# Copying the split Q and K parts and the shift rows straight between SBUF tiles, from two queues, in a two-layer block on one core

## The chip, the cores and the metric

The kernel runs on one core of one Trainium2 chip. The metric is the device time of one execution in microseconds (us); lower is better. Engines are called by the profile's names: PE (TensorE), DVE (VectorE), ACT (ScalarE), POOL (GpSimd), SP (SyncE). SPq and POOLq are the instruction queues from which SP and POOL issue DMAs.

## The reference, cut to what matters

Batch B = 2, sequence S = 512, width D = 128, 16 heads of width 8. Two attentions follow each other for each batch element; both need scores in a precision near float32.

```python
x = x + ffn0(cond_scale(cond, x))                    # quantised feed-forward, inner 512
# first attention: causal, one more key and value made from cond ("image")
q, k, v = split(x @ c_attn_w + c_attn_b)
scores = q k^T / sqrt(8); softmax over 512 keys and the image key
a1 = (softmax @ v) @ c_proj_w + c_proj_b
# second attention: not causal, over a1, then its own projection
q, k, v = split(a1 @ in_proj_w.T + in_proj_b)
a2 = mha(q, k, v) @ out_proj_w.T + out_proj_b
x3 = layernorm(a1 + a2)
out = x + layernorm(x3 + moe(x3))                    # 8 experts, width 256, top 1
```

## The kernel before, in words

The kernel is written by engine: each engine's block walks over one list of steps, ORDER, and executes its share of each step `(name, a, i)`. ORDER is made by `program_order()` from a table of begin, middle and end times written out by hand; within an engine the instructions run in that order. `a` counts the attentions ("instances"): 0 and 1 are the first attention of the two batch elements, 2 and 3 the second; `b = a % 2`. Engines synchronise by semaphores. Line numbers are those of the profile.

**Split into three parts.** Q and K are computed in float32 as 128 rows (8 dims x 16 heads) by 512 positions. Since PE's fast matmul takes bf16, each is split into three bf16 parts: the high part is a cast on ACT (L730 for Q, L736 for K), the middle and low parts are the casts of the rest on DVE (L936 to L938, L942 to L944). They lie in `Qp` and `Kp`, 128 rows by 3 parts by 512.

**Stacks.** A score matmul contracts over 72 rows: three parts of Q times three parts of K times 8 dims. `Qs` holds each part of Q three times in a row (rows 24n to 24n+23 for part n), `Ks` holds the three parts of K in sequence, three times. Each row is one (part pair, dim) and goes over 16 heads by 512 positions. So heads, which are rows in `Qp`, must become columns in `Qs`. Before, that is done by way of DRAM, all of it from SP in the step "v": L514 and L516 write `Qp` and `Kp` (384 KB each) to DRAM tensors; then, for each half of the heads, three DMAs of L526 bring 24 rows each of `Qs`, and three of L533 24 rows each of `Ks` (192 KB each, contiguous runs of 8 KB). That makes 12 DMAs of 192 KB for an instance, 2.36 MB.

**Who waits.** The step "scores" (L1209 on PE) computes 64 score blocks for an instance. Block 0 waits for the first half of the stacks, block 32 for the second half. For each block DVE takes a row maximum (L959). In instance 0 the order runs blocks 0, 1 and 2 and then block 32 as the fourth.

**Shift rows.** From the maxima of 8 heads DVE makes the negated maximum in two bf16 parts, PE transposes it (L1224), ACT copies it to `nmT` (16 rows by 512, L739). SP sends it to DRAM (L538), waits until it is there, and brings it into rows 72 and 73 of `Qs` (L540). Attention of those 8 heads ("attend", L1235) waits for that.

**Rows 72 to 76 at the start.** 14 small DMAs from SBUF to SBUF (L504 to L509, 1 KB runs, one to three destination rows each, 320 KB in all, issued from 22.35 to 33.25 us) fill the constant rows of the stacks in the step "prepare".

Of the kernel before, what the change touches and what calls it, by code (L numbers as in the profile page):

```python
# [17 lines left out]
P = 128  # L18
# [20 lines left out]
INST = 4  # L39
# [187 lines left out]
def two_layers(nc, A, out):  # L227
# [17 lines left out]
    with ctx:  # L245
# [6 lines left out]
        def sem(name):  # L252
            return ctx.enter_context(nc.semaphore(name))


        parts_dram = [[nc.dram_tensor(f"parts_{n}{a}", (PARTS, P, S), bf16, kind="Internal").ap()
                       for n in "qk"] for a in range(INST)]
        shift_dram = [nc.dram_tensor(f"shift_{a}", (2, HEADS, S), bf16, kind="Internal").ap()
                      for a in range(INST)]


        ident = sb("ident", [P, P])
        identb = sb("identb", [P, P], bf16)
        causal_q = sb("causal_q", [P, P], bf16)
# [170 lines left out]
        y_ready = sem("y_ready")  # L435
        r2_ready = sem("r2_ready")
        qhi_ready, khi_ready = sem("qhi_ready"), sem("khi_ready")
        qp_ready, kp_ready = sem("qp_ready"), sem("kp_ready")
        parts_q = [sem(f"parts_q{a}") for a in range(INST)]
        parts_k = [sem(f"parts_k{a}") for a in range(INST)]  # L440
        stacked = [[sem(f"stacked{a}_{n}") for n in range(2)] for a in range(INST)]
        mparts_ready, bias_ready = sem("mparts_ready"), sem("bias_ready")
        half_done = sem("half_done")
        fixed_rows = sem("fixed_rows")
# [1 line left out]
        nm_ready = sem("nm_ready")  # L446
        simg_ready, pimg_ready, zimg_ready = sem("simg_ready"), sem("pimg_ready"), sem("zimg_ready")
        turned_ready, residual_ready = sem("turned_ready"), sem("residual_ready")
        shift_out = [sem(f"shift_out{a}") for a in range(INST)]
        shifted = [[sem(f"shifted{a}_{g}") for g in range(2)] for a in range(INST)]  # L450
        ve_ready, rstd_ready, gained = sem("ve_ready"), sem("rstd_ready"), sem("gained")
        x3_ready = sem("x3_ready")
        dl_ready, ex_ready = sem("dl_ready"), sem("ex_ready")
        comb_ready = sem("comb_ready")
        out_ready, stored = sem("out_ready"), sem("stored")

        block = ctx.enter_context(nc.Block())

# [2 lines left out]
        def _(sp):  # L461
            for step, a, i in ORDER:
# [47 lines left out]
                                     orow[:, :].unsqueeze(1).to_broadcast([PARTS, HEADS, S])).then_inc(fixed_rows, 16)  # L510
                if step == "v":

                    sp.wait_ge(qp_ready, a + 1)
                    sp.dma_start(parts_dram[a][0].rearrange("n p s -> p n s"), Qp[:, :, :]).then_inc(parts_q[a], 16)  # L514
                    sp.wait_ge(kp_ready, a + 1)
                    sp.dma_start(parts_dram[a][1].rearrange("n p s -> p n s"), Kp[:, :, :]).then_inc(parts_k[a], 16)  # L516


                    row, count = HEADS * S, HEADS // 2 * S
                    for half in range(2):  # L520
                        heads = slice(half * HEADS // 2, (half + 1) * HEADS // 2)
                        sp.wait_ge(parts_q[a], 16)
                        for n in range(PARTS):
                            r = n * PARTS * HD
                            src = parts_dram[a][0][n]
                            sp.dma_start(Qs[r:r + PARTS * HD, b, heads, :].rearrange("p h s -> p (h s)"),  # L526
                                         bass.AP(tensor=src.tensor, offset=src.offset + half * count,
                                                 ap=[[0, PARTS], [row, HD], [1, count]])).then_inc(stacked[a][half], 16)
                        sp.wait_ge(parts_k[a], 16)
                        src = parts_dram[a][1]  # L530
                        for n in range(PARTS):
                            r = n * PARTS * HD
                            sp.dma_start(Ks[r:r + PARTS * HD, b, heads, :].rearrange("p h s -> p (h s)"),  # L533
                                         bass.AP(tensor=src.tensor, offset=src.offset + half * count,
                                                 ap=[[row, PARTS * HD], [1, count]])).then_inc(stacked[a][half], 16)
                if step == "max_rows":
                    sp.wait_ge(free["misc"], filled("misc", "max_rows", a, i))
                    sp.dma_start(shift_dram[a][i], nmT[:, b, i, :]).then_inc(shift_out[a], 16)  # L538
                    sp.wait_ge(shift_out[a], 16 * (i + 1))
                    sp.dma_start(Qs[SHIFT:SHIFT + 2, b, i * HALF:(i + 1) * HALF, :].rearrange("p h s -> p (h s)"),  # L540
                                 shift_dram[a][i].rearrange("(n h) s -> n (h s)", h=HALF)).then_inc(shifted[a][i], 16)
                if step == "load_experts":

                    sp.wait_ge(full["t1"], filled("t1", "weights", 2, UNITS - 1))
# [10 lines left out]
        def _(pool):  # L555
# [9 lines left out]
            for step, a, i in ORDER:  # L565
# [44 lines left out]
                if step == "turn_weights":  # L610

                    pool.wait_ge(r1_ready, 1)
                    pool.wait_ge(in_mask, 16)
                    then_wait(pool.tensor_scalar(mparts[:, 0, :], mrow[:, :], 1.0, None, ALU.mult))
                    then_wait(pool.tensor_tensor(mres[:, :], mrow[:, :], mparts[:, 0, :], ALU.subtract))
                    then_wait(pool.tensor_scalar(mparts[:, 1, :], mres[:, :], 1.0, None, ALU.mult))
                    pool.tensor_tensor(mparts[:, 2, :], mres[:, :], mparts[:, 1, :], ALU.subtract)\
                        .then_inc(mparts_ready, 1)
                    pool.wait_ge(in_att, 16 * 17)
                    pool.tensor_tensor(brow[:, 2, :], brow[:, 2, :], brow[:, 3, :], ALU.add)\  # L620
                        .then_inc(bias_ready, 1)
                if step == "max_rows" and a < 2:

                    pool.wait_ge(pimg_ready, NTH[step, a, i])
                    pool.wait_ge(perm_ready, 1)
                    pool.wait_ge(free["s0"], filled("s0", "image_v"))
                    heads, shape = slice(i * HALF, (i + 1) * HALF), [P, NT, HALF, HD + 1]
                    pool.tensor_tensor(Zimg[:, b, :, heads, :], Vimg[:, b, heads, :].unsqueeze(1).to_broadcast(shape),
                                       Pimg[:, b, :, heads].unsqueeze(3).to_broadcast(shape),
                                       ALU.mult).then_inc(zimg_ready, 1)  # L630
# [13 lines left out]
        def _(act):  # L644
# [4 lines left out]
            for step, a, i in ORDER:  # L649
# [70 lines left out]
                if step == "q":  # L720
                    if a >= 1:

                        act.wait_ge(parts_q[a - 1], 16)
                        act.wait_ge(parts_k[a - 1], 16)
                    act.wait_ge(perm_ready, 1)
                    ps = take("misc", "q", a)
                    act.activation(Qf[:, b, :], ps[:, :], ACT.Identity, bias=cols5[:, 0:1] if a < 2 else bjoin[:, 0:1],
                                   scale=float(HD) ** -0.5).then_inc(free["misc"], 1)
                    act.wait_ge(free["misc"], filled("misc", "q", a))
                    act.activation(Qp[:, 0, :], Qf[:, b, :], ACT.Copy).then_inc(qhi_ready, 1)  # L730
# [49 lines left out]
        def _(dve):  # L780
# [39 lines left out]
            for step, a, i in ORDER:  # L820
# [112 lines left out]
                if step == "q":  # L933

                    dve.wait_ge(qhi_ready, a + 1)
                    then_wait(dve.tensor_tensor(qres[:, :], Qf[:, b, :], Qp[:, 0, :], ALU.subtract))  # L936
                    then_wait(dve.tensor_copy(Qp[:, 1, :], qres[:, :]))
                    dve.tensor_tensor(Qp[:, 2, :], qres[:, :], Qp[:, 1, :], ALU.subtract).then_inc(qp_ready, 1)  # L938
                if step == "k":

                    dve.wait_ge(khi_ready, a + 1)
                    then_wait(dve.tensor_tensor(kres[:, :], Kf[:, :], Kp[:, 0, :], ALU.subtract))  # L942
                    then_wait(dve.tensor_copy(Kp[:, 1, :], kres[:, :]))
                    dve.tensor_tensor(Kp[:, 2, :], kres[:, :], Kp[:, 1, :], ALU.subtract).then_inc(kp_ready, 1)  # L944
                if step == "v":
                    if a < 2:
                        dve.wait_ge(stack_init, 2)
# [126 lines left out]
        def _(pe):  # L1074
# [6 lines left out]
            for step, a, i in ORDER:  # L1081
# [114 lines left out]
                        mm = pe.matmul(ps[:, t * D:(t + 1) * D], x[:, b, t * P:(t + 1) * P], w, start=True, stop=True)  # L1196
                    mm.then_inc(full["misc"], 1)
                if step == "scores":
                    if i == HEADS * NT // 2:
                        pe.wait_ge(stacked[a][1], 16 * 2 * PARTS)  # L1200
                    if i == 0:
                        pe.wait_ge(stacked[a][0], 16 * 2 * PARTS)
                        if a < 2:
                            pe.wait_ge(fixed_rows, 16 * 2 * (PARTS + 3))
                    rows = MASK + PARTS if a < 2 else STACK
                    h, t = i // NT, i % NT
                    ps = put(SCORES[a, i], "scores", a, i)
# [153 lines left out]
```

## Time and profile before

| | |
|---|---|
| Time, median of 3 runs | 475.95 us (471.48 to 479.54) |
| Profiled execution, span from the first to the last instruction | 480.0 us |
| Busy in the span | PE 361.9, DVE 257.0, ACT 172.7, POOL 28.7 us |
| Share of the chain that ended last | PE 53%, DVE 15%, DMA 14% |
| Bytes moved by DMA | 18.59 MB |

No other time is given for the profiled execution; its span of 480.0 us lies 0.85% above the median of the runs. Busy time tells how long an engine executed, not what held it up; what held it up is in the waits and in the chain of work that ended last.

### The profile page before, as it was taken

What the parts mean: (1) busy time and instruction counts of PE and PEld (TensorE: products, weight loads), DVE (VectorE), ACT (ScalarE), POOL (GpSimd) and SP (SyncE); (2) the same over time, 40 slices, a digit from 0 to 9 for tenths busy, and PEclk for the clock granted to TensorE, in tenths of its full rate; (3) what the DMA queues carried; (4) which work ended last, traced back from release to release, by engine and by line L of the source; (5) the groups of instructions that cost most, each with busy time, mean ns of one, the idle gap of its engine ahead of it and who ended that gap; (6) DMA issues with size and microseconds to landing.
All of it is one profiled execution on the core that took longest, in us unless ns stands there. A gap on an engine that the chain in (4) does not pass through costs nothing.

```text
span 480.0 us, 5378 instructions
## 1 busy us (share of the span) xinstructions
PE 361.9 (75%) x2027; PEld 176.0 (37%) x2028; DVE 257.0 (54%) x630; ACT 172.7 (36%) x245; POOL 28.7 (6%) x52
## 2 busy tenths in 40 slices
PE   0358633698599987719978947999969999688992
PEld 0134221254345443304322312222433535465771
DVE  4672841699367552204598634567755223336644
ACT  2542320201234456604511751465625674112120
POOL 9600000000000000000000000000010000100000
PEclk9996575657579897955995885589988999869898
DMA  6210441061000000530000251000500000000000
GB/s 179 27 25 2 115 94 55 33 145 72 18 1 3 5 0 4 136 88 41 1 0 4 79 118 68 3 0 18 161 0 4 1 0 1 0 1 1 22 1 22
DMA packets 12092, 18.59 MB, mean 39 GB/s; under 512 B 1261, under 2 KB 10193, under 8 KB 10899
## 3 DMA queue, kind: packets, MB, share of 16 engines
q1 hardware_dynamic: 11778, 17.98, 13.9%
q0 software_dynamic: 288, 0.28, 0.6%
q8 instruction: 16, 0.26, 0.2%
q14 instruction: 10, 0.07, 0.1%
HBM read 14.13 MB, written 3.80 MB: 37 GB/s over the span
## 4 chain that ended last, share of the span: by engine, by line
PE 53%; DVE 15%; DMA 14%; issue 8%; ACT 5%; SPq 3%; POOL 0%; POOLq 0%; DVEq 0%; ACTq 0%
PE ps_pv L1253 11%; DMA Ks<-parts_k 11%; PE ps_t L1235 9%; PE ps_s L1209 9%; DVE mx L959 6%; PE ps_s L1322 4%; PE ps_misc L1330 4%; DMA shift<-nmT 2%; SPq L526 2%; PE ps_misc L1187 2%; PE ps_misc L1264 1%; PE ps_t L1238 1%; ACT probs L764 1%; PE ps_t L1209 1%; PE ps_s L1212 1%
## 5 line engine op out<-in xcount | busy, mean ns | idle before, releaser
L959 DVE TENSOR_REDUCE mx<-ps_s 128x1 f32<-128x512 f32 (+3 forms) x219 | 121.9, 585 | 96.7 <-PE ps_s L1209 59.1
L764 ACT ACTIVATE probs<-ps_t 128x1024 f32<-128x1024 f32 (+2 forms) x128 | 107.8, 864 | 115.0 <-PE ps_t L1238 62.8
L1209 PE MATMUL ps_s<-Ks,Qs 72*128 72x512 bf16 (+4 forms) x219 | 88.4, 428 | 50.2 <-DMA Ks<-parts_k 34.1
L1235 PE MATMUL ps_t<-Qs,Ks 74*128 74x512 bf16 (+4 forms) x256 | 81.5, 392 | 7.4 <-DMA Qs<-shift 5.2
L1209 PEld LDWEIGHTS ps_s<-Ks,Qs 72*128 72x128 bf16 (+1 forms) x219 | 23.6, 111 | 120.7 <-DVE mx L959 53.6
L1253 PE MATMUL ps_pv<-probs,Vs 128*32 128x512 f32 (+3 forms) x512 | 65.6, 589 | 1.4 <-ACT probs L764 1.4
L1235 PEld LDWEIGHTS ps_t<-Qs,Ks 77*128 77x128 bf16 (+1 forms) x256 | 27.0, 110 | 46.8 <-issue 24.0
L1330 PE MATMUL ps_misc<-Ks,shared 128*128 128x128 f32 x256 | 34.6, 292 | 6.2 <-DVE shared L810 2.8
L1330 PEld LDWEIGHTS ps_misc<-Ks,shared 128*128 128x128 f32 x256 | 33.1, 205 | 12.4 <-issue 10.9
L1060 DVE SCALAR_TENSOR_TENSOR shared<-ps_misc,comb,shared 128x128 f32<-128x128 f32 x64 | 18.0, 344 | 32.6 <-PE ps_misc L1330 32.6
L1322 PE MATMUL ps_s<-Qf,Ks 128*128 128x512 f32 x64 | 31.8, 621 | 0.0
L1238 PE MATMUL ps_t<-causal_k,identb 128*128 128x128 bf16 x128 | 28.0, 245 | 0.0
L1212 PE MATMUL ps_s<-causal_q,identb 128*128 128x128 bf16 x100 | 26.1, 265 | 0.0
L750 ACT ACTIVATE shared<-ps_s,cols 128x512 f32<-128x512 f32 x16 | 11.0, 687 | 39.7 <-PE ps_s L1322 39.7
L634 POOL TENSOR_TENSOR rstd<-ve,halves 128x4 f32<-128x4 f32 x4 | 4.2, 1040 | 286.6 <-DVE ve L804 286.6
L739 ACT ACTIVATE nmT<-ps_misc 16x512 bf16<-16x512 bf16 x8 | 4.7, 585 | 43.4 <-PE ps_misc L1224 43.4
L959 DVE TENSOR_REDUCE mx<-ps_t 128x1 f32<-128x512 f32 (+3 forms) x37 | 20.2, 585 | 0.0
L1253 PEld LDWEIGHTS ps_pv<-probs,Vs 128*32 128x32 f32 x512 | 11.1, 113 | 22.5 <-issue 20.4
L1051 DVE TENSOR_SCALAR shared<-ps_s,cols 128x512 f32<-128x512 f32 x16 | 11.9, 746 | 13.3 <-PE ps_s L1322 13.3
L1209 PE MATMUL ps_t<-Ks,Qs 77*128 77x512 bf16 (+4 forms) x37 | 16.1, 463 | 1.5 <-DVE mx L959 1.0
L1322 PEld LDWEIGHTS ps_s<-Qf,Ks 128*128 128x128 f32 x64 | 12.0, 206 | 9.7 <-issue 9.4
L1238 PEld LDWEIGHTS ps_t<-causal_k,identb 128*128 128x128 bf16 x128 | 14.3, 112 | 2.4 <-issue 1.8
(237 smaller groups left out, 348.8 us busy)
## 6 DMA issues: line engine op xcount, KB each, us to landing
Qs<-parts_q SPq DMA_DIRECT2D x24, 192.0 KB
Ks<-parts_k SPq DMA_DIRECT2D x24, 192.0 KB
parts_q<-Qp SPq DMA_DIRECT2D x4, 384.0 KB, 2.5
parts_k<-Kp SPq DMA_DIRECT2D x4, 384.0 KB, 2.6
Ks<-in_L_ffn_w SPq DMA_DIRECT2D x1, 1024.0 KB, 5.8
X<-in_x SPq DMA_DIRECT2D x2, 256.0 KB, 4.3
out_x<-shared SPq DMA_DIRECT2D x2, 256.0 KB, 2.3
shared<-in_L_ffn_w_gate SPq DMA_DIRECT2D x1, 256.0 KB, 4.8
```

The lines of the kernel that those rows point to most:

```text
L750: act.activation(hid[:, i % 2, 1, :], ps[:, :], ACT.Relu, bias=cols17[:, 2 * i + 1:2 * i + 2])\
L764: act.activation(probs[:, half % 2, j, 0:w], ps[:, 0:w], ACT.Exp).then_inc(free[f"t{i % 2}"], 1)
L959: dve.tensor_reduce(mx[:, b, t, h:h + 1], ps[:, 0:w], AX, ALU.max).then_inc(free[SCORES[a, i]], 1)
L1051: dve.tensor_scalar(hid[:, i % 2, 0, :], ps[:, :], cols17[:, 2 * i:2 * i + 1], 0.0, ALU.add, ALU.max).then_inc(free["s0"], 1)
L1060: last = dve.scalar_tensor_tensor(out=acc[:, a, t, :], in0=ps[:, t * D:(t + 1) * D], scalar=comb[:, a, t, i // 2, i % 2:i % 2 + 1], in1=ac ...
L1209: mm = pe.matmul(ps[:, 0:w], Qs[0:rows, b, h, t * P:(t + 1) * P], Ks[0:rows, b, h, 0:w], start=True, stop=(a >= 2))
L1212: mm = pe.matmul(ps[:, w - P:w], identb[:, :], causal_q[:, :], start=False, stop=True)
L1235: mm = pe.matmul(ps[:, col:col + w], Ks[0:rows, b, h, kb * P:(kb + 1) * P], Qs[0:rows, b, h, S - w:S], start=True, stop=(a >= 2))
L1238: mm = pe.matmul(ps[:, col:col + P], identb[:, :], causal_k[:, :], start=False, stop=True)
L1253: mm = pe.matmul(ps[j * HC:(j + 1) * HC, S - w:S], Vs[:, b, kb, r * GROUP + j, :], probs[:, half % 2, j, col:col + w], start=(kb == 0), st ...
L1322: pe.matmul(ps[:, :], W1[:, i, h * P:(h + 1) * P], X3T[:, a, :], start=True, stop=True)\
L1330: mm = pe.matmul(ps[:, t * D:(t + 1) * D], hid[:, i % 2, h, t * P:(t + 1) * P], W2[:, i, h, :], start=(h == 0), stop=(h == FH - 1))
```

## The change: what it does

The DRAM tensors go away. Each part goes from `Qp` or `Kp` into the stacks by three DMAs from SBUF to SBUF, one for each 8-row block in which it stands: 128 source rows of 1 KB become 8 destination rows of 16 runs of 1 KB (128 KB a DMA). An instance has 18 such DMAs, again 2.36 MB. SP issues the nine of Q, POOL the nine of K. The high part's three go as soon as ACT has made it, the others as DVE makes them. The stacks are no longer halved by heads: block 0 of the scores waits for all 18, and nothing waits at block 32. ACT's overwriting of `Qp` in the next instance waits for the 18 DMAs too. The shift rows go from `nmT` to `Qs` in one DMA of 16 KB. Line numbers of the changed kernel are a few lower.

```diff
                 if step == "v":
-                    sp.wait_ge(qp_ready, a + 1)
-                    sp.dma_start(parts_dram[a][0].rearrange("n p s -> p n s"), Qp[:, :, :]).then_inc(parts_q[a], 16)
-                    sp.wait_ge(kp_ready, a + 1)
-                    sp.dma_start(parts_dram[a][1].rearrange("n p s -> p n s"), Kp[:, :, :]).then_inc(parts_k[a], 16)
-                    row, count = HEADS * S, HEADS // 2 * S
-                    for half in range(2):
-                        heads = slice(half * HEADS // 2, (half + 1) * HEADS // 2)
-                        sp.wait_ge(parts_q[a], 16)
-                        for n in range(PARTS):
-                            r = n * PARTS * HD
-                            src = parts_dram[a][0][n]
-                            sp.dma_start(Qs[r:r + PARTS * HD, b, heads, :].rearrange("p h s -> p (h s)"),
-                                         bass.AP(tensor=src.tensor, offset=src.offset + half * count,
-                                                 ap=[[0, PARTS], [row, HD], [1, count]])).then_inc(stacked[a][half], 16)
...
+                    for n in range(PARTS):
+                        if n == 0:
+                            sp.wait_ge(qhi_ready, a + 1)
+                        else:
+                            sp.wait_ge(qrest_ready, a * (PARTS - 1) + n)
+                        for other in range(PARTS):
+                            r = (n * PARTS + other) * HD
+                            sp.dma_start(Qs[r:r + HD, b, :, :], by_rows(Qp, n)).then_inc(stacked[a][0], 16)
                 if step == "max_rows":
                     sp.wait_ge(free["misc"], filled("misc", "max_rows", a, i))
-                    sp.dma_start(shift_dram[a][i], nmT[:, b, i, :]).then_inc(shift_out[a], 16)
-                    sp.wait_ge(shift_out[a], 16 * (i + 1))
-                    sp.dma_start(Qs[SHIFT:SHIFT + 2, b, i * HALF:(i + 1) * HALF, :].rearrange("p h s -> p (h s)"),
-                                 shift_dram[a][i].rearrange("(n h) s -> n (h s)", h=HALF)).then_inc(shifted[a][i], 16)
+                    sp.dma_start(Qs[SHIFT:SHIFT + 2, b, i * HALF:(i + 1) * HALF, :], shift_rows(b, i))\
+                      .then_inc(shifted[a][i], 16)
...
+                if step == "v":
+
+                    for n in range(PARTS):
+                        if n == 0:
+                            pool.wait_ge(khi_ready, a + 1)
+                        else:
+                            pool.wait_ge(krest_ready, a * (PARTS - 1) + n)
+                        for other in range(PARTS):
+                            r = (other * PARTS + n) * HD
+                            pool.dma_start(Ks[r:r + HD, b, :, :], by_rows(Kp, n)).then_inc(stacked[a][1], 16)
...
                     if a >= 1:
 
-                        act.wait_ge(parts_q[a - 1], 16)
-                        act.wait_ge(parts_k[a - 1], 16)
+                        for n in range(2):
+                            act.wait_ge(stacked[a - 1][n], 16 * PARTS * PARTS)
...
                 if step == "scores":
-                    if i == HEADS * NT // 2:
-                        pe.wait_ge(stacked[a][1], 16 * 2 * PARTS)
                     if i == 0:
-                        pe.wait_ge(stacked[a][0], 16 * 2 * PARTS)
+                        for n in range(2):
+                            pe.wait_ge(stacked[a][n], 16 * PARTS * PARTS)
```

The two new access patterns:

```python
def by_rows(parts, n):      # part n: 128 rows, 512 elements each
    ap = parts[:, n, :]
    return bass.AP(tensor=ap.tensor, offset=ap.offset, ap=[[PARTS * S, P], [1, S]])

def shift_rows(b, i):       # 16 rows of nmT, 512 elements each
    ap = nmT[:, b, i, :]
    return bass.AP(tensor=ap.tensor, offset=ap.offset, ap=[[2 * 2 * S, HEADS], [1, S]])
```

How the instructions stand on SP around the stacks of instance 1 and the first shift rows of instance 0, before (a row with x2 stands for two like it; the last two numbers are rows by elements of the tile written):

```order
L514 DMA parts_q<-Qp 128x3x512 [waits qp_ready]
L516 DMA parts_k<-Kp 128x3x512 [waits kp_ready]
L526 DMA Qs<-parts_q 24x1x4096 [waits parts_q1]
L526 DMA Qs<-parts_q 24x1x4096 x2
L533 DMA Ks<-parts_k 24x4096 [waits parts_k1]
L533 DMA Ks<-parts_k 24x4096 x2
L526 DMA Qs<-parts_q 24x1x4096 [waits parts_q1]
L526 DMA Qs<-parts_q 24x1x4096 x2
L533 DMA Ks<-parts_k 24x4096 [waits parts_k1]
L533 DMA Ks<-parts_k 24x4096 x2
L538 DMA shift<-nmT 16x512 [waits misc_free]
L540 DMA Qs<-shift 2x4096 [waits shift_out0]
```

The same place on SP now:

```order
L521 DMA Qs<-Qp 8x16x512 [waits qhi_ready]
L521 DMA Qs<-Qp 8x16x512 x2
L521 DMA Qs<-Qp 8x16x512 [waits qrest_ready]
L521 DMA Qs<-Qp 8x16x512 x2
L521 DMA Qs<-Qp 8x16x512 [waits qrest_ready]
L521 DMA Qs<-Qp 8x16x512 x2
L524 DMA Qs<-nmT 2x8x512 [waits misc_free] x4
```

SP issues nine DMAs in place of fourteen, the first of them after the high part alone; the shift rows stand behind the stacks of instance 1 in both.

On POOL, from the end of the setup (`brow` is a bias row) to the first work of the attentions (`Zimg`, the image key's share), before:

```order
L616 TENSOR_SCALAR shared<-shared 2x512 [waits pool_step]
L617 TENSOR_TENSOR shared<-shared 2x512 [waits pool_step]
L620 TENSOR_TENSOR brow<-brow 1x128 [waits in_att]
L628 TENSOR_TENSOR Zimg<-Vimg,Pimg 128x4x72 [waits s0_free,perm_ready,pimg_ready] x4
L634 TENSOR_TENSOR rstd<-ve,halves 128x4 [waits ve_ready]
```

and now, with the first nine of the two instances' 18:

```order
L604 TENSOR_TENSOR brow<-brow 1x128 [waits in_att]
L615 DMA Ks<-Kp 8x16x512 [waits khi_ready]
L615 DMA Ks<-Kp 8x16x512 x2
L615 DMA Ks<-Kp 8x16x512 [waits krest_ready]
L615 DMA Ks<-Kp 8x16x512 x2
L615 DMA Ks<-Kp 8x16x512 [waits krest_ready]
L615 DMA Ks<-Kp 8x16x512 x2
```

The K stacks of instances 0 and 1 went in ahead of POOL's `Zimg`, those of 2 and 3 behind it and ahead of the first `rstd`.

On PE at the first four score blocks of instance 0, before:

```order
L1209 MATMUL ps_s<-Ks,Qs 128x128 [waits s0_free,fixed_rows,stacked0_0]
L1212 MATMUL ps_s<-causal_q,identb 128x128
L1209 MATMUL ps_s<-Ks,Qs 128x256 [waits s1_free]
L1212 MATMUL ps_s<-causal_q,identb 128x128
L1209 MATMUL ps_s<-Ks,Qs 128x384 [waits s0_free]
L1212 MATMUL ps_s<-causal_q,identb 128x128
L1209 MATMUL ps_s<-Ks,Qs 128x128 [waits s1_free,stacked0_1]
```

and now:

```order
L1204 MATMUL ps_s<-Ks,Qs 128x128 [waits fixed_rows,s0_free,stacked0_k,stacked0_q]
L1207 MATMUL ps_s<-causal_q,identb 128x128
L1204 MATMUL ps_s<-Ks,Qs 128x256 [waits s1_free]
L1207 MATMUL ps_s<-causal_q,identb 128x128
L1204 MATMUL ps_s<-Ks,Qs 128x384 [waits s0_free]
L1207 MATMUL ps_s<-causal_q,identb 128x128
L1204 MATMUL ps_s<-Ks,Qs 128x128 [waits s1_free]
```

The order of the matmuls is the same; the wait for the second half of the heads moved from the fourth block into the first.

## Rows read from the trace of the kernel before

**Rows 1.** Waits of PE over the whole span: us in total, times, longest us

```profile
PE ps_s L1209 <- DMA Ks<-parts_k: 34.1, 4, 12.3
PE ps_t L1235 <- DMA Qs<-shift: 5.2, 1, 5.2
```

**Rows 2.** Timeline of PE: start us, us, instruction, in brackets idle before and releaser

```profile
66.59 0.66 PE L1173 MATMUL ps_misc<-ident,X 128*128 128x128 f32 x4 [1.22 <-DVE X L929]
72.58 0.29 PE L1209 MATMUL ps_s<-Ks,Qs 77*128 77x128 bf16 x1 [5.33 <-DMA Ks<-parts_k]
...
73.65 0.31 PE L1212 MATMUL ps_s<-causal_q,identb 128*128 128x128 bf16 x1
81.66 0.29 PE L1209 MATMUL ps_s<-Ks,Qs 77*128 77x128 bf16 x1 [7.69 <-DMA Ks<-parts_k]
...
114.80 0.31 PE L1209 MATMUL ps_t<-Ks,Qs 77*128 77x128 bf16 x1
...
119.86 0.31 PE L1212 MATMUL ps_s<-causal_q,identb 128*128 128x128 bf16 x1
125.34 0.61 PE L1235 MATMUL ps_t<-Qs,Ks 77*128 77x512 bf16 x1 [5.17 <-DMA Qs<-shift]
...
214.24 1.03 PE L1209 MATMUL ps_s<-Ks,Qs 72*128 72x512 bf16 x2 [12.35 <-DMA Ks<-parts_k]
...
290.64 0.61 PE L1209 MATMUL ps_s<-Ks,Qs 72*128 72x512 bf16 x1 [8.70 <-DMA Ks<-parts_k]
```

**Rows 3.** Timeline of SP's queue, issues of instances 0, 1 and 2 and first shift

```profile
53.22 2.20 SPq L526 DMA_DIRECT2D Qs<-parts_q  x3
...
59.16 1.32 SPq L533 DMA_DIRECT2D Ks<-parts_k  x3
...
115.01 0.31 SPq L538 DMA_DIRECT2D shift<-nmT  x1
123.53 0.22 SPq L540 DMA_DIRECT2D Qs<-shift  x1
...
195.52 2.56 SPq L526 DMA_DIRECT2D Qs<-parts_q  x3
```

**Rows 4.** Timelines of ACT and DVE where the parts are made

```profile
47.36 0.63 ACT L730 ACTIVATE Qp<-Qf 128x512 bf16<-128x512 f32 x1
50.22 0.63 ACT L736 ACTIVATE Kp<-Kf 128x512 bf16<-128x512 f32 x1
52.07 0.69 DVE L944 TENSOR_TENSOR Kp<-kres,Kp 128x512 bf16<-128x512 f32 x1
85.24 0.63 ACT L730 ACTIVATE Qp<-Qf 128x512 bf16<-128x512 f32 x1
188.91 0.63 ACT L730 ACTIVATE Qp<-Qf 128x512 bf16<-128x512 f32 x1
266.93 0.63 ACT L730 ACTIVATE Qp<-Qf 128x512 bf16<-128x512 f32 x1
```

**Rows 5.** Four windows: stretch, us, busy by engine, PE clock, DMA share, GB/s

```profile
26.00:31.00 5.00, 0.34 (x1) 0.00 (x0) 3.88 (x11) 1.90 (x3) 0.00 (x0) 1.00 0.17 26
51.00:52.00 1.00, 0.00 (x0) 0.13 (x2) 0.97 (x2) 0.55 (x1) 0.00 (x0) 0.50 1.02 341
57.00:65.00 8.00, 4.54 (x37) 3.66 (x37) 6.51 (x18) 3.21 (x5) 0.00 (x0) 0.71 0.74 143
66.00:80.00 14.00, 1.98 (x10) 0.90 (x10) 1.81 (x6) 0.60 (x1) 0.00 (x0) 0.62 0.19 73
```

**Rows 6.** DMA issues by line: KB each, median us to landing; POOL's issue in its timeline

```profile
norm_gb<-in_L_ffn_ln_g POOLq DMA_DIRECT2D x2, 64.0 KB, 3.4
shift<-nmT SPq DMA_DIRECT2D x8, 16.0 KB, 1.4
...
12.93 0.56 POOL L609 DMA_DIRECT2D norm_gb<-in_L_ffn_ln_b  x1
```

More of the change, by code:

```diff
@@ L253, in sem @@
             return ctx.enter_context(nc.semaphore(name))
[L256 to L259, printed above, removed]
         ident = sb("ident", [P, P])
@@ L437, in two_layers @@
         qhi_ready, khi_ready = sem("qhi_ready"), sem("khi_ready")
[L438 to L441, printed above, removed]
+        qrest_ready, krest_ready = sem("qrest_ready"), sem("krest_ready")
+        stacked = [[sem(f"stacked{a}_{n}") for n in "qk"] for a in range(INST)]
         mparts_ready, bias_ready = sem("mparts_ready"), sem("bias_ready")
@@ L448, in two_layers @@
         turned_ready, residual_ready = sem("turned_ready"), sem("residual_ready")
-        shift_out = [sem(f"shift_out{a}") for a in range(INST)]
         shifted = [[sem(f"shifted{a}_{g}") for g in range(2)] for a in range(INST)]
@@ L511, in _ @@
                 if step == "v":
-                    sp.wait_ge(qp_ready, a + 1)
-                    sp.dma_start(parts_dram[a][0].rearrange("n p s -> p n s"), Qp[:, :, :]).then_inc(parts_q[a], 16)
-                    sp.wait_ge(kp_ready, a + 1)
-                    sp.dma_start(parts_dram[a][1].rearrange("n p s -> p n s"), Kp[:, :, :]).then_inc(parts_k[a], 16)
-                    row, count = HEADS * S, HEADS // 2 * S
-                    for half in range(2):
-                        heads = slice(half * HEADS // 2, (half + 1) * HEADS // 2)
-                        sp.wait_ge(parts_q[a], 16)
-                        for n in range(PARTS):
-                            r = n * PARTS * HD
-                            src = parts_dram[a][0][n]
-                            sp.dma_start(Qs[r:r + PARTS * HD, b, heads, :].rearrange("p h s -> p (h s)"),
-                                         bass.AP(tensor=src.tensor, offset=src.offset + half * count,
-                                                 ap=[[0, PARTS], [row, HD], [1, count]])).then_inc(stacked[a][half], 16)
[L529 to L535, printed above, removed]
@@ L936, in _ @@
                     then_wait(dve.tensor_tensor(qres[:, :], Qf[:, b, :], Qp[:, 0, :], ALU.subtract))
-                    then_wait(dve.tensor_copy(Qp[:, 1, :], qres[:, :]))
-                    dve.tensor_tensor(Qp[:, 2, :], qres[:, :], Qp[:, 1, :], ALU.subtract).then_inc(qp_ready, 1)
+                    dve.tensor_copy(Qp[:, 1, :], qres[:, :]).then_inc(qrest_ready, 1)
+                    dve.wait_ge(qrest_ready, a * (PARTS - 1) + 1)
+                    dve.tensor_tensor(Qp[:, 2, :], qres[:, :], Qp[:, 1, :], ALU.subtract).then_inc(qrest_ready, 1)
                 if step == "k":
@@ L942, in _ @@
                     then_wait(dve.tensor_tensor(kres[:, :], Kf[:, :], Kp[:, 0, :], ALU.subtract))
-                    then_wait(dve.tensor_copy(Kp[:, 1, :], kres[:, :]))
-                    dve.tensor_tensor(Kp[:, 2, :], kres[:, :], Kp[:, 1, :], ALU.subtract).then_inc(kp_ready, 1)
+                    dve.tensor_copy(Kp[:, 1, :], kres[:, :]).then_inc(krest_ready, 1)
+                    dve.wait_ge(krest_ready, a * (PARTS - 1) + 1)
+                    dve.tensor_tensor(Kp[:, 2, :], kres[:, :], Kp[:, 1, :], ALU.subtract).then_inc(krest_ready, 1)
                 if step == "v":
```

## The prediction

> **What bounds the kernel now.** I read the waits of PE first. PE waits for the K stacks four times, 34.1 us in all, and once for the shift rows, 5.2 us [rows 1]; nothing else that the edit touches holds PE. The timeline of PE gives the places [rows 2]: instance 0, 5.33 us up to 72.58 (first half of the heads) and 7.69 us up to 81.66 (second half); instance 2, 12.35 us up to 214.24; instance 3, 8.70 us up to 290.64. Instance 1's stacks are in time: its block 0 runs at 114.80 without a wait; but the first shift rows of instance 0, issued at 115.01, take 8.5 us for the way out alone (123.53) where the median of eight is 1.4 [rows 3, 6], because they queue behind those stacks, and attention starts at 125.34 after 5.17 us of idling [rows 2]. In these five places PE, ACT and DVE all run dry, so each us won or lost there goes into the span. The most that can be won is 39.3 us.
>
> **How fast stacks are filled.** This decides everything, so the windows come next [rows 5]. DMA share times 16 gives the busy DMA engines. (a) 66 to 80 us, only Q's DMAs left: 0.19, three engines, 73 GB/s, 24 GB/s each. (b) 57 to 65, Q and K: 0.74, twelve engines, 143 GB/s, 12 GB/s each. Twelve engines are each half as fast as three, so the engines aren't the limit in (b). (c) 26 to 31, the constant rows, SBUF to SBUF in 1 KB runs into one to three destination rows: 0.17, 2.7 engines, 26 GB/s, under 10 each. (d) 51 to 52, a part written from 128 rows to DRAM in 1 KB runs: all engines, 341 GB/s, 21 each; short runs alone aren't slow. What (b) and (c) share is few destination rows: 24 rows took 143 GB/s, 6 GB/s a row; five neighbouring rows took 26. A DMA of the change writes 8 rows. Bounds: 8 x 6 = 48 GB/s from (b); two groups of rows at 26 each, 52, from (c). I take 50: 131 KB / 50 = 2.6 us a DMA. As to engines, a Q DMA of before (3 copies of 8 rows) used three, a K DMA of 24 rows twelve; for 8 rows I read eight, half of them.
>
> The Trainium skill says why (SBUF — State Buffer, "Door 1: The DMA port swizzle"): four neighbouring rows share a port of about 27 GB/s, so 8 rows get 54. Our 26 and 143 (24 rows, six ports) agree. By its figure a DMA takes 2.4 us, each stack comes 2 us earlier, and the forecast below would be 478 instead of 486.
>
> **The stack, part by part.** Removed: the two writes to DRAM and the wait for both (from 47.99, when Q's high part is made, to 53.22, the first stack DMA: 5.2 us in instance 0 [rows 3, 4]). Added: 18 DMAs of 2.6 us. SP's issues take 0.73 each (2.20 / 3 [rows 3]), nine are 6.6 us; POOL's 0.56 [rows 6], nine are 5 us: both hidden behind the transfers. Nine DMAs of Q one after another: 23.6 us, and 1.4 to land [rows 6]: 25 us after Q's high part, at best. K's nine start 2 to 7 us later in another queue. If both queues shared each engine's time fully, it would be 18 x 2.6 + 1.4 = 48 us. Between them: if half of K's DMAs fall on the eight engines that Q leaves free, the other eight carry 13.5 DMAs, 35 us, and since the queues write different rows at the same moment part of that overlaps. I take 31 us from Q's high part to the last landing, 29.6 of transfer or 80 GB/s: nearest to the row of before, where 2.36 MB took from 53.22 to 81.66 [rows 2, 3], 83 GB/s. Bounds 25 and 48.
>
> **Place by place**, with 31 us:
> - Instance 0: Q high at 47.99, complete at 79.0, against 81.66; but blocks 0 to 2, which ran from 72.58 to 73.96 in the wait [rows 2], now come after it, 1.5 us. Change -1.2.
> - Instance 1: Q high at 85.87, complete at 116.9. Block 0 was due at 114.80: a new wait of 2.1, where there was none. The stretch from 114.80 to 120.17 follows, attention starts at 122.3 instead of 125.34. The shift rows go in one hop and find Q's queue empty by 117, so their wait is gone. Change -3.0. What is late next is that stack.
> - Instance 2: Q high at 189.54, complete at 220.5. Before, block 0 needed only the first half, landed at 214.24. Change +6.3.
> - Instance 3: Q high at 267.56, complete at 298.6 against 290.64. Change +8.0.
>
> The last two lose because the half that let PE start is gone: before, half the heads came 18.7 us after the first issue (195.52 to 214.24 [rows 2, 3]), and the rest landed behind work.
>
> The remaining edits: the seven other shift hops save about 1.7 us each (1.4 and an issue), behind scores and attention, where PE never waits for them [rows 1]: nothing; with that cover gone they would be a gain. ACT's wait before the next Q asks for stacks that PE has already waited for before it makes that Q: nothing. On POOL the K issues stand where it has nothing else queued between `brow` and `Zimg`; `Zimg` comes behind those of instance 1, which end some 5 us after K's parts, well before the first maxima: nothing. DVE's split of the last increment is the same three instructions.
>
> Sum: -1.2 - 3.0 + 6.3 + 8.0 = +10.1 on the span of 480.0, 490.1; scaled to the median of the runs (475.95 / 480.0), **486 us**.
>
> **Rivals.**
> 1. *The two queues don't disturb each other.* The stack is complete 25 us after Q's high part. Instance 0: 73.0, -7.2; instance 1: 110.9, no wait, shift rows in time, -5.1; instance 2: 214.5, +0.3; instance 3: 292.6, +2.0. Sum -10.0, **466 us**. For it: four engines could each give 21 GB/s by (d), while their four rows take 26 in all by (c), so they have time over for another queue's rows. Against: it needs K's stream to finish no later than Q's, though it starts later.
> 2. *The eight engines serve both queues by turns, and a write that waits for its rows holds the other queue.* With 13.5 DMAs in sequence, 36.5 us: +4.3, +2.5, +11.8, +13.5, sum +32, **508 us**; with all 18, 48 us: +15.8, +14.0, +23.3, +25.0, 553 us. It decides from about 30 us of filling on. For it: in (b) engines were held to half their speed for 8 us with Q's and K's DMAs on three of them together.
> 3. *Destination rows aren't the limit* and (b) and (c) were slow for another reason (reading DRAM, three copies of one source). Then eight engines at 21 GB/s from (d) fill 131 KB in 0.8 us, issuing decides, and instance 0's stack is there at 52.76 + 3 x 0.56 + 3.4 = 57.8, before PE is ready at 67.25 [rows 2, 4, 6]. All waits but the blocks' 1.5 us go: -12.9, -5.1, -12.3, -8.7, sum -39, **437 us**. Against: (c) is SBUF to SBUF with the same runs and still gets 26 GB/s.
>
> Beside rival 2 stands a rule of the Trainium skill (DMA: Bandwidth & Descriptors, "Rules for kernel authors" and "Back-pressure in remote DMA"): issuing from several engines saves only issue time, since all DMAs run on the same 16 engines, and stalled writes stall an engine's other queues too. No row here shows two queues at once; by the rule rival 2 or my middle value holds, not rival 1. The same page has POOL's DMAs take their engines from a cursor that moves on, which no row here shows.
>
> **How the numbers follow.** Forecast 0.43, rival 1 0.23, rival 2 0.22, rival 3 0.10, other 0.02. The forecast's own range is 478 to 497. The range of 8 in 10 takes in rival 1 with a little margin and the milder rival 2: 464 to 512; rival 3 and the worse end of rival 2 are left out. Two per cent, what a measurement of this kernel tells from no change, are 466.4 and 485.5. Faster: rival 3 and half of rival 1, 0.22. Slower: rival 2 and some six tenths of the forecast's case, 0.48. Same: the rest, 0.30.
>
> **What would show it.** Right: during the filling a DMA share near 0.5 at 50 GB/s while Q is alone (instance 1, between 86.5 and 93), and 70 to 90 GB/s with K; waits of PE for the stacks in all four instances, 116 to 118 for instance 1; no wait for shift rows. Wrong: 100 GB/s or more with one queue (rival 3), 100 with both (rival 1), 55 with both (rival 2); a POOL issue far above 0.56 us would be a cause that I don't have.

## The result and the profile after

The changed kernel takes 497.69 us in the median (490.87 to 505.60, four runs), beside 476.32 us for the kernel before (471.48 to 479.54): ratio 1.039, 95% interval 1.027 to 1.051. It is slower by 4%. The forecast was 486 in a range of 464 to 512. Runs of one kernel spread by some per cent, the longer ones as a rule at a lower granted clock of PE, so the ratio leaves the slowest out, and since the profiled execution of the changed kernel (span 497.0, clock 0.79, against 480.0 at 0.80) is one of these, the two profiles are compared place by place below.

Waits of PE in the changed kernel, as in [rows 1]:

```profile
PE ps_s L1204 <- DMA Qs<-Qp: 54.9, 3, 21.4
...
PE ps_t L1204 <- issue: 3.6, 1, 3.6
```

The four waits for K's stacks (34.1 us) are now three waits of 54.9 and one of 3.6 that the profile can't name; its place (instance 1's block 0, below) says that it is for the stack. The wait for the shift rows is gone. Together 58.5 us where there were 39.3: 19 us more, against 17.0 in the span. The same places in PE's timeline as in [rows 2]:

```profile
82.09 0.29 PE L1204 MATMUL ps_s<-Ks,Qs 77*128 77x128 bf16 x1 [14.71 <-DMA Qs<-Qp]
...
121.81 0.27 PE L1204 MATMUL ps_t<-Ks,Qs 77*128 77x128 bf16 x1 [3.60 <-issue]
...
126.93 0.63 PE L1230 MATMUL ps_t<-Qs,Ks 77*128 77x512 bf16 x1
...
221.74 1.03 PE L1204 MATMUL ps_s<-Ks,Qs 72*128 72x512 bf16 x2 [21.38 <-DMA Qs<-Qp]
...
307.93 0.61 PE L1204 MATMUL ps_s<-Ks,Qs 72*128 72x512 bf16 x1 [18.76 <-DMA Qs<-Qp]
```

ACT's timeline, where Q's high parts are made (start, us), to be set beside [rows 4]; the first is at 47.48, where it was at 47.36:

```profile
87.50 0.63 ACT L724 ACTIVATE Qp<-Qf 128x512 bf16<-128x512 f32 x1
...
187.38 0.63 ACT L724 ACTIVATE Qp<-Qf 128x512 bf16<-128x512 f32 x1
...
274.15 0.63 ACT L724 ACTIVATE Qp<-Qf 128x512 bf16<-128x512 f32 x1
```

From the end of that cast to block 0 it is 34.0, 33.7, 33.7 and 33.2 us in the four instances. Before, it was 24.6 (instance 0), 24.7 (instance 2) and 23.1 (instance 3) to the first half [rows 2, 4]; to both halves it was 33.7 in instance 0 (47.99 to 81.66), as long as now. The windows of the changed kernel, columns as in [rows 5] (Q and K together in instance 0; Q alone in instance 1; mostly both in instance 1):

```profile
57.00:64.00 7.00, 3.63 (x30) 3.03 (x30) 6.21 (x17) 3.34 (x5) 0.00 (x0) 0.74 1.09 100
90.00:95.00 5.00, 4.71 (x17) 2.42 (x18) 3.22 (x9) 0.93 (x2) 0.00 (x0) 0.50 0.58 68
99.00:116.00 17.00, 16.34 (x85) 9.94 (x86) 15.24 (x38) 0.00 (x0) 1.99 (x4) 0.60 0.92 83
```

With two queues the share stands near or above 1.0, and yet it is 83 to 100 GB/s, where the same share moved 341 GB/s into DRAM before [rows 5]: engines that wait, not engines that move. POOL's issuing doesn't hold this up: an issue takes 0.60 us (median) and the nine stand back to back, but a K DMA takes 14.2 us to land (median of 36) where POOL's DMAs of 64 KB at the start take 3.1 to 3.2.

### The profile page after: what moved, and what is told of

It is laid out like the page before. It is cut to its first block, busy times and chain, and to the rows that moved or that the text cites. A ratio compares the mean times of both kernels' runs of the same rounds, so it can differ in the third digit from the quotient of the medians.

```text
span 497.0 us, 5385 instructions
## 1 busy us (share of the span) xinstructions
PE 360.1 (72%) x2028; PEld 177.2 (36%) x2028; DVE 257.1 (52%) x630; ACT 172.5 (35%) x245; POOL 50.3 (10%) x88
## 4 chain that ended last, share of the span: by engine, by line
PE 51%; DMA 18%; DVE 13%; issue 9%; ACT 5%; SPq 3%; POOL 0%; POOLq 0%; DVEq 0%; ACTq 0%
DMA Qs<-Qp 17%; PE ps_pv L1248 10%; PE ps_s L1204 9%; PE ps_t L1230 9%; DVE mx L955 6%; PE ps_s L1317 4%; PE ps_misc L1325 4%; SPq L521 3%; PE ps_t L1204 1%; PE ps_misc L1259 1%; PE ps_misc L1183 1%; PE ps_t L1233 1%; PE ps_s L1207 1%; ACT probs L758 1%; DMA X<-in_x 1%
## 5 line engine op out<-in xcount | busy, mean ns | idle before, releaser
L1204 PE MATMUL ps_s<-Ks,Qs 72*128 72x512 bf16 (+4 forms) x219 | 87.9, 426 | 70.5 <-DMA Qs<-Qp 54.9
L1230 PE MATMUL ps_t<-Qs,Ks 74*128 74x512 bf16 (+4 forms) x256 | 78.4, 380 | 3.1 <-ACT probs L758 2.9
L1248 PE MATMUL ps_pv<-probs,Vs 128*32 128x512 f32 (+3 forms) x512 | 63.9, 576 | 1.4 <-ACT probs L758 1.4
L1230 PEld LDWEIGHTS ps_t<-Qs,Ks 77*128 77x128 bf16 (+1 forms) x256 | 26.4, 107 | 39.8 <-issue 20.4
L1325 PE MATMUL ps_misc<-Ks,shared 128*128 128x128 f32 x256 | 35.8, 299 | 6.2 <-DVE shared L804 2.8
L1325 PEld LDWEIGHTS ps_misc<-Ks,shared 128*128 128x128 f32 x256 | 34.3, 212 | 12.4 <-issue 10.9
L615 POOL DMA_DIRECT2D Ks<-Kp x36 | 21.5, 605 | 155.8 <-ACT Kp L730 155.8
L744 ACT ACTIVATE shared<-ps_s,cols 128x512 f32<-128x512 f32 x16 | 11.0, 687 | 42.6 <-PE ps_s L1317 42.6
L1204 PE MATMUL ps_t<-Ks,Qs 77*128 77x512 bf16 (+4 forms) x37 | 17.1, 491 | 4.9 <-issue 3.6
L1248 PEld LDWEIGHTS ps_pv<-probs,Vs 128*32 128x32 f32 x512 | 10.9, 112 | 22.7 <-issue 19.7
## 6 DMA issues: line engine op xcount, KB each, us to landing
Ks<-Kp POOLq DMA_DIRECT2D x36, 128.0 KB, 14.2
```

The source lines that it names most:

```text
L615: pool.dma_start(Ks[r:r + HD, b, :, :], by_rows(Kp, n)).then_inc(stacked[a][1], 16)
L1230: mm = pe.matmul(ps[:, col:col + w], Ks[0:rows, b, h, kb * P:(kb + 1) * P], Qs[0:rows, b, h, S - w:S], start=True, stop=(a >= 2))
L1248: mm = pe.matmul(ps[j * HC:(j + 1) * HC, S - w:S], Vs[:, b, kb, r * GROUP + j, :], probs[:, half % 2, j, col:col + w], start=(kb == 0), st ...
L1325: mm = pe.matmul(ps[:, t * D:(t + 1) * D], hid[:, i % 2, h, t * P:(t + 1) * P], W2[:, i, h, :], start=(h == 0), stop=(h == FH - 1))
```

## The experiments

"Stack" below is the time from the end of Q's high part on ACT to block 0 of the scores. Each run had the kernel before beside it on the same chip. Where neither an interval nor a number of runs is given, the time is that of one run; stacks are read from the traces.

**1. What was the lost half worth?** The kernel before with this edit:

```diff
                     if i == 0:
                         pe.wait_ge(stacked[a][0], 16 * 2 * PARTS)
+                        pe.wait_ge(stacked[a][1], 16 * 2 * PARTS)
```

> The kernel before, with one line more: block 0 of the scores waits for the second half of the stacks too; the copies by way of DRAM stay. Theory A (most of the loss is the lost half of the heads, the direct copies themselves are about as slow as the old way): instance 0 +1.5 to 2, instance 1 a wait of some 5 to 8 us at block 0 that shortens the shift wait by as much, instances 2 and 3 +9.5 each (28.4 us for all in place of 18.7), sum about +20, 496 us. Theory B (the direct copies themselves cost the time): nearly no change, under +5 us.

Measured: ratio 1.052 (1.040 to 1.063), median 504.77 beside 481.37. In its timeline of PE:

```profile
81.50 0.27 PE L1210 MATMUL ps_s<-Ks,Qs 77*128 77x128 bf16 x1 [13.09 <-issue]
124.01 0.27 PE L1210 MATMUL ps_t<-Ks,Qs 77*128 77x128 bf16 x1 [7.89 <-issue]
...
227.38 1.01 PE L1210 MATMUL ps_s<-Ks,Qs 72*128 72x512 bf16 x2 [22.09 <-issue]
...
311.81 0.59 PE L1210 MATMUL ps_s<-Ks,Qs 72*128 72x512 bf16 x1 [17.65 <-DMA Ks<-parts_k]
```

Theory A holds. One semaphore wait, moved from block 32 to block 0, costs 5%, no less than the whole change does (4%). Its stacks take 32.0 to 36.5 us, the changed kernel's 33.2 to 34.0: once everything is waited for, both ways are about as slow, and the 5.2 us of the hop that the direct copies save are lost again in their transfers (in instance 0, 26.7 us from the first to the last packet of the stack there, 31.4 in the changed kernel). The two intervals overlap, so whether the direct copies gave anything back isn't settled by the times.

**2. Which limit fills a stack?** Only the order of the 72 rows in both stacks is changed; the contraction doesn't depend on it. Q's side of the edit, K's is the same:

```diff
+        def stack_rows(m):
+            return slice(m, m + 9 * (HD - 1) + 1, 9)
...
-                            r = (n * PARTS + other) * HD
-                            sp.dma_start(Qs[r:r + HD, b, :, :], by_rows(Qp, n)).then_inc(stacked[a][0], 16)
+                            sp.dma_start(Qs[stack_rows(n * PARTS + other), b, :, :], by_rows(Qp, n)).then_inc(stacked[a][0], 16)
```

> The changed kernel with the 72 rows of both stacks in another order: block m of 8 rows takes rows m, m+9, ..., m+63 instead of 8m to 8m+7, so each DMA writes rows nine apart. Same DMAs, queues, bytes and runs. Theory A (neighbouring rows in groups of four take 26 GB/s together): a DMA reaches eight groups, eight engines at 21 GB/s take 0.8 us for it, and from Q's high part to the first scores it takes 8 to 12 us where it was 34; all waits of PE for stacks but 0 to 3 us go, the span is 445 to 455. Theory B (eight engines, two queues on the same engines, or runs of 1 KB are the limit): still 33 to 34 us, no change of time.

Measured: median 447.20 (438.36 to 452.77, four runs) beside 481.37, instance 0's block 0 without a wait, instance 3's stack 16.4 us (241.80 to 258.16), all that is left of the waits of PE for DMAs:

```profile
PE ps_s L1206 <- issue: 3.0, 1, 3.0
PE ps_s L1206 <- DMA Qs<-Qp: 2.0, 1, 2.0
```

The same bytes, runs and queues in half the time: theory A, the rows. The stack (17.1 us in instance 2) is above the 8 to 12 that I gave. As an estimate from [rows 5], eight engines at 21 GB/s need 14 us for the 2.36 MB of a stack; that limit I had named but not summed.

**3 and 4. How do rows share?** Two more orders, four groups of rows a DMA, and eight groups in pairs 32 rows apart:

```diff
         def stack_rows(m):
-            return slice(m, m + 9 * (HD - 1) + 1, 9)
+            if m == 8:
+                return slice(64, 72)
+            r = m // 2 * 16 + m % 2
+            return slice(r, r + 2 * (HD - 1) + 1, 2)
```

```diff
         def stack_rows(m):
-            return slice(m, m + 9 * (HD - 1) + 1, 9)
+            if m == 8:
+                return slice(64, 72)
+            return slice(m, m + 8 * (HD - 1) + 1, 8)
```

> As the one before, but the rows of a block are two apart (0, 2, ..., 14 and 1, 3, ..., 15, and so on; the ninth block stays on rows 64 to 71): a DMA reaches four groups of four rows. Theory A: 104 GB/s a DMA, 1.26 us, the stack about 17 to 19 us, the span about 460 to 465. Theory B: 34 us, no change.

> As the one before, but the rows of a block are eight apart (m, m+8, ..., m+56; the ninth block on rows 64 to 71), so a DMA reaches eight different groups of four rows, but these are four pairs that lie 32 rows apart. If each group of four has its own 26 GB/s: as with rows nine apart, 8 to 12 us a stack. If groups 32 rows apart share it, as the Trainium skill has it (SBUF — State Buffer, Door 1): as with rows two apart, 17 to 19 us. Theory B: 34 us.

Measured: 453.45 and 470.82 us, one run each. The waits of PE for stacks are nearly the same, 21.8 and 22.7 us in all, so what parts the two times isn't in the stacks; PE's clock is 0.83 in the one and 0.80 in the other. Stacks: 21.6 to 23.8 us with rows two apart (three instances that wait), 22.3 to 25.7 with rows eight apart, 16 to 18 nine apart, 33 to 34 side by side. The cleanest comparison is the stretch of instance 1 in which only Q's DMAs run, from one queue, here with rows nine, two and eight apart:

```profile
76.00:81.00 5.00, 4.95 (x18) 2.41 (x18) 2.98 (x7) 1.18 (x2) 0.00 (x0) 0.50 0.53 173
```

```profile
80.00:85.00 5.00, 5.00 (x18) 2.39 (x18) 2.91 (x7) 1.25 (x2) 0.00 (x0) 0.50 0.56 108
```

```profile
81.00:86.00 5.00, 4.54 (x18) 1.74 (x17) 3.34 (x8) 1.32 (x2) 0.25 (x1) 0.66 0.56 104
```

With the same eight or nine engines busy, 173, 108 and 104 GB/s, and 68 side by side (window 90 to 95 above; 58 in a longer stretch, experiment 5). So eight groups in pairs 32 apart are no better than four groups: groups 32 rows apart share what they may take, as the Trainium skill has it (SBUF — State Buffer, "Door 1: The DMA port swizzle"). The 104 GB/s expected of four groups is what came. The stacks are 3 to 7 us longer than expected all the same; the ninth block, left on rows 64 to 71, is one part of that, the rest isn't worked out. The order of the four cases is as expected.

**5. What was the second queue worth?** All 18 DMAs from SP, the body of POOL's loop moved behind Q's:

```diff
+                    for n in range(PARTS):
+                        if n == 0:
+                            sp.wait_ge(khi_ready, a + 1)
+                        else:
+                            sp.wait_ge(krest_ready, a * (PARTS - 1) + n)
+                        for other in range(PARTS):
+                            r = (other * PARTS + n) * HD
+                            sp.dma_start(Ks[r:r + HD, b, :, :], by_rows(Kp, n)).then_inc(stacked[a][1], 16)
```

> The changed kernel with all 18 DMAs of an instance issued by SP, Q's nine and then K's nine; POOL issues none. Rows as in the changed kernel, eight neighbours a DMA. Theory C (a DMA of 8 neighbouring rows takes 2.3 to 2.6 us whatever is queued, and the second queue was worth an overlap): one after another, 41 to 47 us from Q's high part to the first scores in every instance, and a span of 530 to 550. Theory D (the second queue is worth nothing, all share the same engines and rows): 33 to 35 us as with two queues, the span within 1% of 497.

Measured: 528.88 us. Its window, and block 0 of instance 0 in PE's timeline:

```profile
57.00:64.00 7.00, 3.74 (x32) 2.89 (x31) 5.54 (x17) 2.93 (x4) 0.00 (x0) 0.50 0.57 58
```

```profile
89.61 0.27 PE L1202 MATMUL ps_s<-Ks,Qs 77*128 77x128 bf16 x1 [22.81 <-issue]
```

The stack is 42.6 us in instance 0 (46.98 to 89.61), 42.4, 39.8 and 42.6 in the others. Share 0.57 is nine engines at 58 GB/s, 6.4 each; 131 KB take 2.26 us. Theory C: the second queue is worth 6 to 9 us a stack and, by one run, some 30 us of the time.

**6. The shift rows by themselves.** The kernel before with the changed kernel's one DMA for L538 and L540:

```diff
-                    sp.dma_start(shift_dram[a][i], nmT[:, b, i, :]).then_inc(shift_out[a], 16)
-                    sp.wait_ge(shift_out[a], 16 * (i + 1))
-                    sp.dma_start(Qs[SHIFT:SHIFT + 2, b, i * HALF:(i + 1) * HALF, :].rearrange("p h s -> p (h s)"),
-                                 shift_dram[a][i].rearrange("(n h) s -> n (h s)", h=HALF)).then_inc(shifted[a][i], 16)
+                    sp.dma_start(Qs[SHIFT:SHIFT + 2, b, i * HALF:(i + 1) * HALF, :], shift_rows(b, i))\
+                      .then_inc(shifted[a][i], 16)
```

> The kernel before with the shift rows copied straight from the one SBUF tile to the other, and nothing else changed. Theory E (the 8.5 us of the first shift were queueing behind the stacks of instance 1, the way out being 1.4 us otherwise): attention of instance 0 still starts about 124 to 125.5 where it was 125.34, the other seven save 1.4 us each that nobody waits for, the time is the same within 1.5 us. Rival: the hop itself costs, 5 us at that place and more behind it, 468 to 472 where the kernel before has 476.

Measured: 484.74 us in the median of four (476.01 to 490.63), beside 477.91 of before (473.08 to 489.16 in seven); with ranges so wide the time tells nothing apart. The place does:

```profile
123.14 0.61 PE L1238 MATMUL ps_t<-Qs,Ks 77*128 77x512 bf16 x1 [3.47 <-DMA Qs<-nmT]
```

Issued at 114.50, the one DMA still isn't there before 123: it queues behind the stacks of instance 1, as the two did (125.34). From the issue to attention it is 8.6 us where it was 10.3 (115.01 to 125.34), 1.7 less, about one hop (1.4 us and an issue). Theory E; attention starts a little before the 124 to 125.5 that I gave.

**7. One queue with the rows nine apart.** Experiment 2 with K's DMAs from SP as in 5.

> Rows nine apart and all 18 DMAs issued by SP. With rows nine apart a DMA takes 0.8 us on eight engines and SP's issue 0.61 to 0.73: 18 x 0.8 = 15 us of filling from Q's high part if K's follow without a gap, so about as long as the 15 us with two queues (theory C: there two queues share engines). Then the time is within 1% of the one with two queues. If the second queue's use of other engines is what counts, 18 us or more, and 5 to 10 us slower.

Measured: ratio 0.942 (0.925 to 0.958), median 453.75, stacks of 18.5 and 18.8 us (instances 2 and 3) against 16.4 to 18.0 with two queues. Its window:

```profile
51.00:59.00 8.00, 5.66 (x16) 2.65 (x16) 7.05 (x12) 3.35 (x5) 0.00 (x0) 0.50 0.55 171
```

Nearly the same share as in 5 (0.55 and 0.57), nine engines, and three times the bytes: 19 GB/s each, close to the 21 of the part written to DRAM [rows 5]. Once rows are spread, one queue's engines are the limit, and the second queue is worth 0.5 to 2.4 us a stack and nothing that the ratios tell (0.943 with two, experiment 9). With both queues on spread rows (experiment 2, window 56 to 60) the share is 1.06 and the rate 195 GB/s, hardly more than 171, so there engines aren't the limit either; what is, no run here parts.

**8. Where does a second queue get its overlap?** K's nine DMAs issued by ACT.

> The changed kernel with K's nine DMAs issued by ACT in place of POOL; rows as in the changed kernel. It asks where the overlap of two queues comes from. If from POOL's DMAs running on other engines than SP's (shares above 1.0 of all 16 were read with both): ACT's queue uses the same eight engines as SP's, the DMA share stays near 0.5 to 1.0 and the filling takes 36 to 44 us. If from two queues writing different rows at once on the same engines: 31 to 34 us as with POOL. ACT also spends 9 x 0.7 = 6 us an instance on issuing, beside its exponentials.

Measured: 510.89 us. The stack takes 39.9 and 39.7 us in instances 0 and 1 and 35.7 in the last two, between the changed kernel's 33 to 34 and the 40 to 43 of one queue. Where both queues move data (302 to 315 us, instance 3), the window and the two queues' shares are:

```profile
302.00:315.00 13.00, 7.17 (x20) 1.64 (x20) 2.77 (x4) 5.01 (x5) 0.00 (x0) 0.50 0.56 85
```

```profile
q10 hardware_dynamic: 595, 0.57, 29.3%
q1 hardware_dynamic: 541, 0.52, 26.7%
```

Here q1 is SP's queue and q10 ACT's. The two shares add up to 0.56, about what SP's queue has alone in experiment 5 (0.57): SP's and ACT's DMAs run on the same nine or so engines. And still it is 85 GB/s and not 58: two queues that write different rows overlap on the same engines too, almost as much as with POOL's (83 to 100). What is lost is at the start. ACT's K DMAs begin to move 8 to 10 us after ACT's first issue. From 204 to 213 us, for example, ACT issues eight of the nine and all the data that moves is of SP's queue (share 0.57). POOL's begin 1 to 3 us after its first issue. In instance 0 ACT also issues 6 us late, behind its other work. Until they overlap, the rate is that of one queue.

The time is not the stack's alone. ACT's nine issues take 12 to 17 us and not the 6 expected, and PE's waits for stacks are 31.1 us in all (58.5 in the changed kernel), but those for ACT at attention have grown from 2.9 us to 31.2:

```profile
PE ps_t L1229 <- ACT probs L757: 31.2, 6, 15.0
```

So a second queue gains even where it has no engines of its own. The reading that fits is that two DMAs write different rows at the same time. Shares up to 1.09 with POOL's queue say that its DMAs run at least in part on other engines than SP's, and these don't stand in line behind them. Neither this reading nor why ACT's stand in line was tested by itself.

**9. The best version again**, the kernel of experiment 2, for its interval.

> Rows nine apart, Q from SP and K from POOL, the same kernel as the first one with that order of rows, for an interval of its time. From its profile (451 us at a PE clock of 0.81, 447 median) against the kernel before: ratio 0.92 to 0.95, filling of a stack again 15 us, waits of PE for stacks 3 to 6 us in all.

Measured: ratio 0.943 (0.930 to 0.956), median 446.59 (440.64 to 448.38) beside 480.41. The waits of PE for stacks are 7.3 us, a little above the 3 to 6 given, and the stacks take 18.0 and 17.8 us, above the 15. The kernel before and the changed one (ratio 1.039) are both beaten.

**10. Is the direct way needed?** The kernel before, by way of DRAM and from SP alone, with spread rows and one wait:

```diff
+                    row = HEADS * S
+                    for n in range(2):
+                        sp.wait_ge((parts_q, parts_k)[n][a], 16)
+                        for m in range(PARTS * PARTS):
+                            src = parts_dram[a][n][m // PARTS if n == 0 else m % PARTS]
+                            dst = (Qs, Ks)[n]
+                            sp.dma_start(dst[m:m + 9 * (HD - 1) + 1:9, b, :, :].rearrange("p h s -> p (h s)"),
+                                         bass.AP(tensor=src.tensor, offset=src.offset,
+                                                 ap=[[row, HD], [1, row]])).then_inc(stacked[a][n], 16)
```

> The kernel before, still by way of DRAM and all from SP, shift rows too, but each stack is filled by 18 DMAs of 8 rows nine apart (runs of 16 KB, 128 KB a DMA), and block 0 waits for all 18 since the halves are gone. If the spread of the rows is what speeds things up and the direct way saves only the hop: the stack takes the 5.2 us of the hop more than the direct one, 20 to 22 us from Q's high part to the first scores; a wait of PE of 3 to 5 us in instance 0, about 5 in instance 2 and 7 in instance 3, the time 455 to 465. If the direct way is what counts once rows are spread: 28 us or more, 475 or above.

Measured: ratio 0.976 (0.964 to 0.988), median 460.48. The stack is 21.1 us in instance 0, 22.3 in instance 2 and 20.5 in instance 3.

```profile
57.00:64.00 7.00, 3.84 (x29) 3.20 (x28) 6.14 (x18) 3.45 (x5) 0.00 (x0) 0.50 0.51 191
```

Eight engines (0.51) at 23 GB/s each, a fifth more than the 19 of experiment 7 with its runs of 1 KB. Against experiment 1, by way of DRAM with one wait too, the ratio falls from 1.052 to 0.976; the spread rows are in that, and also that Q's DMAs, three engines each before [rows 5], now use eight, which isn't parted here. The direct way adds less: from one queue and with spread rows the ratio goes from 0.976 to 0.942 (experiment 7, the intervals don't touch) and the stack from 20.5 to 22.3 us down to 18.5 to 18.8. Spread rows with the halves kept, so that PE may start early, were not tried.

## Why the prediction was right, and where it was off

- *What bounds the kernel.* Right: the changed waits at the five places (+19 us) answer to the span (+17), but for 3 us outside them, below.
- *Rate of a DMA into 8 neighbouring rows.* I took 50 GB/s from 48 and 52; experiment 5 shows 58, so 2.26 us a DMA, not 2.6. The term was mis-sized by 13%, on the safe side. The mechanism, few destination rows and not runs, engines or issue, is shown by experiments 2 to 5 and 7.
- *Stack of 31 us.* It took 33.2 to 34.0, and that it came so near is in part luck. With 2.26 us a DMA, 18 of them one after another are 40.7 us; the two queues brought it to 31 us or so from first to last byte (30.8 to 31.8 by the packets in the trace, 76 GB/s for the whole), 24% less. I had 18 x 2.6 = 46.8 brought down to 29.6, 37% less: the DMA was taken too slow and the overlap of the two queues too large, and the errors nearly cancelled. With the overlap that I assumed, the faster DMA would have given 26 us of transfer. The overlap rested on no row of two queues. On top of that come 1.3 us from the cast to the first packet and 0.6 to 1.6 us from the last packet to the first matmul, where I had allowed 1.4 in all.
- *Instance 0*: forecast -1.2. Block 0 came at 82.09 for 79.0, and Q's next high part at 87.50 for 85.24: +2.3. The 3 us of the stack are the error. *Instance 1*: attention started at 126.93, +1.6 in all, so -0.7 at this place where I had -3.0. The new wait at block 0 is there, 3.6 us for 2.1, and the shift wait is gone as said. *Instance 2*: 24.7 us became 33.7, +9.0 for +6.3. *Instance 3*: 23.1 became 33.2, +10.1 for +8.0. Between attention of instance 0 and Q of instance 2 the profiled execution gained 3.1 us that no edit explains: PE's clock in 125 to 190 us is 0.88, and 0.82 in the same window before; that this is the cause isn't shown.
- *The sum*: +10.1 forecast, +17.0 in the span; the four places' 2 to 3.5 us each are the difference, less those 3.1.
- *"The last two lose because the half that let PE start is gone"*: shown by experiment 1. That wait alone costs 5% there.
- *Rival 1* (queues don't disturb each other, 466): ruled out by stacks of 33 to 34 us where it wanted 25. Its sign, 100 GB/s with both queues, was met in one window (57 to 64) but not over a stack (76). *Rival 2* (turns on the same engines, 508): not so with POOL's queue. That issuing from a second queue would save issue time only, the rule beside it, doesn't hold here: 58 GB/s with one queue, 83 to 100 with SP and POOL, 85 with SP and ACT on the same engines. The 510.9 of experiment 8 is near 508 by accident: its stacks cost PE less waiting than the changed kernel's (31.1 us against 58.5), and 28 us of new waits for ACT stand beside them. *Rival 3* (rows aren't the limit, 437): wrong for this kernel; with rows spread its time comes near (447), with 5 to 7 us of waits left that its sum didn't have.
- *ACT's new wait, POOL's order, the seven other shift hops at nothing*: no wait of PE or ACT in the changed kernel names them.
- *Signs*: share 0.58 and 68 GB/s while Q is alone (near 0.5 and 50 forecast), 83 to 100 GB/s with both in the windows (70 to 90 forecast), a stack wait in every instance, block 0 of instance 1 at 121.8 (116 to 118 forecast).

## What to carry to other kernels

When a copy fills few rows of SBUF, ask for each DMA which rows it writes at one time, and spread them: the same copies into rows nine apart took half as long, for one slice in the code. Before a path is replaced, look which of its pieces lets the consumer start: the halves that were dropped along with the DRAM hop were worth 5%, and the direct copies didn't win it back. And a DMA share of 1.0 with 90 GB/s means engines that wait, where the same share elsewhere in this kernel moved 341 GB/s; read the share and the GB/s together.

## What the runs showed of the hardware that I had not expected

Groups of four rows that lie 32 rows apart share what they may take: from one queue, eight groups in such pairs took 104 GB/s, four groups 108, eight separate ones 173, two groups 58 to 68. Two queues that write different rows overlapped even on the same engines: SP's and ACT's together had the share of one (0.56) and 85 GB/s where one has 58. SP's and POOL's together had shares up to 1.09, so POOL's DMAs ran at least in part on engines that SP's left free. ACT's K DMAs began 8 to 10 us after their first issue, POOL's 1 to 3. SP's issue of a DMA that runs on eight engines took 0.61 us, of one on all sixteen 0.39. And the order of 72 rows that no result depends on moved the time by 10% (497.69 to 447 us).
